# A gated linear-attention stage on one core: inner states kept by strips of two heads, one copy of the inner gate, variance as two float32r products

## The reference

```
xn = layernorm(x)
# gated linear attention, 16 heads, key size 16, value size 32
y  = rmsnorm(xn) ; q = y@Wq ; k = y@Wk * 32**-0.5 ; v = y@Wv ; g = y@Wg + bg
gk = logsigmoid(y@Wkg1@Wkg2 + bkg2) / 16          # Wkg1 is 512x16: the inner gate
S_t = S_{t-1} * exp(gk_t) + k_t v_t ;  o_t = q_t S_t     # per head, over the tokens
o  = (o - mean(o)) * rsqrt(var(o) + 1e-5)          # per head, over its 32 values
xm = xn + (silu(g) * o) @ Wo
s  = xm + (silu(rmsnorm(xm)@W1) * (rmsnorm(xm)@W3)) @ W2     # hidden size 1408
# a second branch from xn: softmax-weighted low-rank experts, then silu -> gate
out = x + s * gate
```

## Time and profile before

| | |
|---|---|
| median of 3 runs | 1599.29 us (1598.97 to 1599.48) |
| the profiled execution | 1597.72 us |
| its span, first to last instruction | 1596.0 us, granted TensorE clock 0.999 |
| PE busy | 1576.8 us (99%) |
| DVE busy | 847.4 us (53%), in stage A over 80% |
| ACT busy | 567.2 us (36%) |
| PE waits for another engine inside stage A | 0.4 us and 0.2 us |
| PE's wait for DVE's first inner gate, at the end of stage F | 0.19 us |
| from the ms subtraction (L1040) to the o0 addition (L1080), DVE, seven rows | 31.9 to 32.2 us |

### The profile page before, as it was taken

One profiled execution on the slowest core, in us unless ns is written; L12 is line 12 of the kernel. 1 busy time (PEld: TensorE's weight loads), 2 busy tenths in 40 slices (PEclk: granted clock), 3 DMA queues, 4 the chain that ended last, 5 costly groups with the idle time before them and its releaser, 6 DMA issues.

```text
span 1596.0 us, 30636 instructions
## 1 busy us (share of the span) xinstructions
PE 1576.8 (99%) x12274; PEld 1275.5 (80%) x12274; DVE 847.4 (53%) x1320; ACT 567.2 (36%) x988; POOL 162.5 (10%) x190
## 2 busy tenths in 40 slices
PE   7999999999999999999999999999999999999998
PEld 5888787787777777777777888888888888888887
DVE  5554555467797887978887451331415132241513
ACT  4333344276564655736555411111111111111111
POOL 1222331100221102201020100000000000000000
PEclk9999999999999999999999999999999999999999
DMA  7443442101020211202123423030300203030110
GB/s 160 142 101 92 119 112 73 60 28 42 22 87 3 87 43 47 87 3 87 61 82 123 142 96 136 0 138 0 138 0 30 108 0 138 0 138 0 63 44 27
DMA packets 50757, 114.08 MB, mean 71 GB/s; under 512 B 13322, under 2 KB 24666, under 8 KB 42467
## 3 DMA queue, kind: packets, MB, share of 16 engines
q1 hardware_dynamic: 47906, 99.95, 19.3%
q10 hardware_dynamic: 1152, 8.39, 1.3%
q0 software_dynamic: 1600, 4.25, 1.3%
HBM read 78.98 MB, written 33.59 MB: 71 GB/s over the span
## 4 chain that ended last, share of the span: by engine, by line
PE 90%; DVE 6%; ACT 1%; issue 1%; DMA 1%; SPq 1%; DVEq 0%; PEld 0%; ACTq 0%; PEldq 0%
PE m_ps L1569 9%; PE m_ps L1568 9%; PE m_ps L1567 9%; PE a_ps L161 7%; PE a_ps L163 7%; PE a_ps L162 7%; PE f_ps L161 6%; PE f_ps L163 5%; PE f_ps L162 5%; PE m_ps L1589 4%; PE m_ps L1590 4%; PE m_ps L1588 4%; PE a_att L1312 3%; PE a_ps L1431 2%; PE a_ps L1333 2%; DVE row L1843 1%
## 5 line engine op out<-in xcount | busy, mean ns | idle before, releaser
L1817 DVE TENSOR_TENSOR m_h<-m_ps,m_silu 128x512 f32<-128x512 f32 x85 | 58.7, 690 | 392.9 <-PE m_ps L1569 392.9
L1567 PE MATMUL m_ps<-m_xshi,m_w 128*128 128x512 f32 x680 | 266.2, 392 | 0.0
L1569 PE MATMUL m_ps<-m_xshi,m_w 128*128 128x512 f32 x680 | 264.7, 389 | 0.0
L1568 PE MATMUL m_ps<-m_xslo,m_w 128*128 128x512 f32 x680 | 264.6, 389 | 0.0
L1883 ACT ACTIVATE m_silu<-m_ps 128x512 f32<-128x512 f32 x85 | 50.7, 597 | 325.8 <-PE m_ps L1569 325.8
L1569 PEld LDWEIGHTS m_ps<-m_xshi,m_w 128*128 128x128 f32 x680 | 127.6, 188 | 26.6
L1567 PEld LDWEIGHTS m_ps<-m_xshi,m_w 128*128 128x128 f32 x680 | 127.7, 188 | 26.4 <-issue 0.2
L1568 PEld LDWEIGHTS m_ps<-m_xslo,m_w 128*128 128x128 f32 x680 | 127.7, 188 | 26.3 <-issue 0.2
L1045 DVE TENSOR_TENSOR a_a<-a_att,causal 128x1024 f32<-128x1024 f32 x64 | 75.2, 1216 | 11.8 <-PE a_att L1312 11.8
L1893 ACT ACTIVATE m_h0hi<-m_h 128x512 fp32r<-128x512 f32 x45 | 28.5, 633 | 132.0 <-DVE m_h L1817 132.0
L1588 PE MATMUL m_ps<-m_h0hi,m_w 128*128 128x512 f32 x188 | 73.1, 389 | 0.0
(11 more groups left out here) (318 smaller groups left out, 3484.5 us busy)
## 6 DMA issues: line engine op xcount, KB each, us to landing
row<-scratch_xn SPq DMA_DIRECT2D x16, 1024.0 KB, 4.8
row<-scratch_xmid SPq DMA_DIRECT2D x16, 1024.0 KB, 7.3
m_xt<-in_L_attn_W SPq DMA_DIRECT2D x33, 256.0 KB, 3.0
f_xt<-in_L_attn_x SPq DMA_DIRECT2D x32, 256.0 KB, 7.8
scratch_xn<-row SPq DMA_DIRECT2D x8, 1024.0 KB, 8.6
scratch_gate<-row ACTq DMA_DIRECT2D x8, 1024.0 KB, 3.9
scratch_xmid<-row SPq DMA_DIRECT2D x8, 1024.0 KB, 4.9
row<-scratch_gate SPq DMA_DIRECT2D x8, 1024.0 KB, 10.4
```

The costliest lines, as they stand in the source:

```text
L1567: pe.matmul(ps, wh, xh, start=k == 0, stop=False)
L1568: pe.matmul(ps, wh, xl, start=False, stop=False)
L1569: ins = pe.matmul(ps, wl, xh, start=False, stop=k == LAST)
L1817: dve.tensor_tensor(h[n], dense.region(f"b{j}"), silu[n], ALU.mult).then_inc(dense.taken_sem(f"b{j}"), 1)
```

## The change

- **States by strips.** `state` is 128 x 2 x 64 instead of 128 x 2 x 256: a strip of 32 partitions holds the two heads of that strip. State times query becomes eight products of 32 rows x 64 columns at tile positions (32*strip, 64*(strip % 2)), strips 0 and 1 into one bank, 2 and 3 into another. The mix has two banks (`a_mix`), in half of each. DVE's update is one masked copy of 128x128 and two steps of 128x64.
- **Transposed keys** go to the unused half of a mix bank (`turned`). For c = 1 and 2 they are made behind the projection instead of ahead of it, and the state products must wait until ACT has copied them.
- **Inner gate.** The weights hold three copies of the high part, so that four row blocks of u arise at once. ACT makes one copy (64x512), DVE one subtraction; before, DVE made three copies and the subtraction (16x512 each). The preparation of these weights on POOL changes with it.
- **Variance.** ACT squares into `sq`, ACT copies the high part into `og_hl[0]`, DVE subtracts for the low part (`squares_lo`), and TensorE adds two float32r products.
- **Gating.** `gated` is split: `weigh_out(c)` multiplies the silu gate with `oc`, and `gated` has three operations and runs two chunks on. ACT does `deviation` ahead of `inverse_deviation` in chunk 3.
- **Banks.** `dense` has two banks and, through a table `places`, the four attention banks for z, v1, v2, g0, g1, g2. The memsets of the attention banks (`clear_weights`) go. The loop's `head_slot` for TensorE goes.

```diff
-        psum = [... for b in range(4)]
+        psum = [... for b in range(2)]
+        ps_mix = ctx.enter_context(nc.psum_tensor("a_mix", [P, 2, 512], F32))[:]
+        places = {result: n for n, results in enumerate((
+            ["k0", "ds0", "var0", "q0", "ds2", "var2", "var3", "v3", "o0", "o2"],
+            ["k1", "u", "ds1", "var1", "q1", "ms", "v0", "g3", "o1", "o3"],
+            ["z0", "g0"], ["z1", "g1"], ["v1", "g2"], ["v2"])) for result in results}
+        turned = Regions(count, "kt", [ps_mix[:, ODD, GR * P:]], list(range(NC - 1)))
...
# DVE, inner gate
-                dve.tensor_copy(u[0:RANK], ps).then_inc(count.sem("uhi"), 1)
-                dve.tensor_copy(u[64:64 + RANK], ps).then_inc(count.sem("uhi"), 1)
-                dve.tensor_copy(u[96:96 + RANK], at.region("u")[32:32 + RANK]).then_inc(count.sem("uhi"), 1)
                 dve.wait_ge(*count.at("uhi", i))
-                dve.tensor_tensor(u[32:32 + RANK], ps, u[0:RANK].bitcast(F32), ALU.subtract)...
+                dve.tensor_tensor(u[low], at.region("u")[low], u[low].bitcast(F32), ALU.subtract)...
# ACT, inner gate
+                act.activation(u[0:4 * RANK], at.region("u")[0:4 * RANK], ACT.Copy).then_inc(count.sem("uhi"), 1)
# DVE, body
             for c in range(NC):
                 if c > 0:
-                    dve.wait_ge(*mix.ready(c - 1, i))
+                    squares_lo(i, c - 1)
                 ...                                   # ms low part (c = 3), masks, ahead
+                if c > 1:
+                    gated(i, c - 2)
                 ...                                   # state update
                 if c > 0:
-                    gated(i, c - 1)
+                    weigh_out(i, c - 1)
+            gated(i, NC - 2)
+            squares_lo(i, NC - 1)
+            weigh_out(i, NC - 1)
             ahead("gates")
             gated(i, NC - 1)
+        def weigh_out(i, c):
+            part = gsilu[:, :, tokens(c)]
+            dve.wait_ge(*dense.taken(f"g{LAST}", i))
+            dve.wait_ge(*mix.taken(c, i))
+            dve.tensor_tensor(part, part, oc, ALU.mult).then_inc(count.sem("og"), 1)
# ACT, body
+                if c == 1:
+                    squares(i, (2,))
                 for part in (("k0", "k1"), ("u",), ("q0",), ("q1",))[c]:
                     ahead(part)
+                if 0 < c < NC - 1:
+                    keys(i, c)
...
+                if c == NC - 1:
+                    deviation(i)
                 if c > 0:
                     inverse_deviation(i, c - 1)
-                if c == NC - 1:
-                    deviation(i)
                 act.wait_ge(*mix.ready(c, i))
-                act.activation(flat(sq), ps, ACT.Square).then_inc(count.sem("sq"), 1)
+                act.activation(by_quads(sq), ps, ACT.Square).then_inc(count.sem("squares"), 1)
+                act.wait_ge(*count.at("squares", i, 3 * c + 1))
+                act.activation(og_hl[0][:, :, tokens(c)], sq, ACT.Copy).then_inc(count.sem("squares"), 1)
# PE
-                pe.matmul(ps, avg32, flat(sq), start=True, stop=True)...
+                pe.matmul(ps, avg32.bitcast(F32R), og_hl[0][:, :, tokens(c)], start=True, stop=False)
+                pe.matmul(ps, avg32.bitcast(F32R), og_hl[1][:, :, tokens(c)], start=False, stop=True)...
...
+                    if 0 < c < NC - 1:
+                        pe.wait_ge(*mix.taken(c - 1, i))
+                        turned_keys(i, c)
                     if c > 0:
                         variance(i, c - 1)
...
+                    if 0 < c < NC - 1:
+                        pe.wait_ge(*turned.taken(c, i))
-                        for quad in range(QD):
-                            pe.matmul(ps[:, quad, :], state[c % 2][:, g, first_head * VH:...], qhat[:, gcs[g], :], ...)
+                        for g in range(GR):
+                            for strip in range(4):
+                                rows, at = slice(H32 * strip, H32 * (strip + 1)), H64 * (strip % 2)
+                                pe.matmul(ps[2 * g + strip // 2][at:at + H64], state[c % 2][rows, g, :],
+                                          qhat[rows, gcs[g], :], ..., tile_position=(H32 * strip, at))
```

More of the change, by code:

```diff
@@ L58, with __init__ @@
 class Regions:
-    def __init__(self, counts, name, regions, order, early=()):
+    def __init__(self, counts, name, regions, order, early=(), places=None):
         self.counts, self.name, self.regions = counts, name, regions
@@ L169, in loop, with loop_parts @@
     loop_parts(eng, n, {None: first}, lambda i, ahead: body(i, lambda: ahead(None)), peel)
-def loop_parts(eng, n, parts, body, peel=False, before=None, skip=None, first=True, slot=None):
+def loop_parts(eng, n, parts, body, peel=False, before=None, skip=None, first=True):
     for part, work in parts.items() if first else ():
@@ L182, in loop_parts @@
         body(0, lambda part: parts[part](1))
-    with eng.bass.Fori(1 if peel else 0, n - 1, engines=bass.OrderedEngineSet([eng.engine]), hint_back_edge=True,
-                       head_slot=None if slot is None else {eng.engine: slot}) as i:
+    with eng.bass.Fori(1 if peel else 0, n - 1, engines=bass.OrderedEngineSet([eng.engine]), hint_back_edge=True) as i:
         body(i, lambda part: parts[part](i + 1))
@@ L272, in prepare_attention_weights @@
     step(pool.memset(w["wkg2"].bitcast(F32), 0.0))
-    step(pool.memset(w["wkg1"].bitcast(F32), 0.0))
     RANK, KD = Wkg2.shape
-    small = w["stage"][0:RANK, 1, 0:KD]
+    small = w["stage"][0:4 * RANK, 1, 0:KD]
     sources = {"wkg1": Wkg1, "wk": Wk, "wq": Wq, "wv": Wv, "wg": Wg, "wo": Wo}
@@ L827, in phase_a @@
         kt_sb = flat(w["fold"]).rearrange("p (g t) -> p g t", g=GR)
-        state = [sb(f"state{n}", [P, GR, HG * VH]) for n in range(2)]
+        state = [sb(f"state{n}", [P, GR, 2 * VH]) for n in range(2)]
         sq, oc, rn = sb("sq", [P, QD, P]), sb("oc", [P, QD, P]), sb("rn", [P, QD, P])
@@ L845, in phase_a @@
                           ("decay", 1), ("m64", 3), ("m32", 3), ("mdk", 1), ("mdq", 2), ("mkh", 1), ("mqh", 1),
-                          ("state", GR * (NC - 2)), ("first", NC - 1), ("weighing", NC),
-                          ("sq", NC), ("rn", NC), ("og", 2 * NC), ("oghi", NC), ("oglo", NC)):
+                          ("state", GR * (NC - 2)), ("weighing", NC),
+                          ("squares", 3 * NC), ("rn", NC), ("og", 2 * NC), ("oghi", NC), ("oglo", NC)):
             count.add(name, per)
@@ L1218, in deviation, with keys, by_quads @@
                 act.activation(added[0:1], added[0:1], ACT.Exp, scale=-0.5).then_inc(count.sem("r2"), 1)
+            def keys(i, c):
+                act.wait_ge(*turned.ready(c, i))
+                act.activation(flat(kt_sb), turned.region(c), ACT.Copy).then_inc(turned.taken_sem(c), 1)
+            def by_quads(ap):
+                return ap.rearrange("p (g b) t -> p g b t", b=2)
             def body(i, ahead):
@@ L1230, in body @@
-                    for part in (("k0", "k1"), ("c1",), ("q0",), ("q1",))[c]:
+                        act.activation(og_hl[0][:, :, tokens(c)], square, ACT.Copy).then_inc(count.sem("x2parts"), 1)
+                    if c == 1:
+                        squares(i, (2,))
+                    for part in (("k0", "k1"), ("u",), ("q0",), ("q1",))[c]:
                         ahead(part)
+                    if 0 < c < NC - 1:
+                        keys(i, c)
                     if c == 0:
                         act.wait_ge(*dense.taken_before(f"o{LAST}", i))
-                    squares(i, ((0, 1), (2,), (3,), ())[c])
+                        squares(i, (0, 1))
@@ L1275, in first_row @@
                 elif part == "lent":
-                    for name in ("k0", "k1"):
+                    for name in ("u", "k0", "k1"):
                         parts[name](0, first)
@@ L1419, in body @@
                     if c > 0:
-                        for quad in range(QD):
-                            g, first_head = quad * HQ // HG, quad * HQ % HG
-                            pe.matmul(ps[:, quad, :], state[c % 2][:, g, first_head * VH:(first_head + HQ) * VH],
-                                      qhat[:, gcs[g], :], start=quad == 0, stop=True, skip_group_check=True)
+                        for g in range(GR):
+                            for strip in range(4):
+                                rows, at = slice(H32 * strip, H32 * (strip + 1)), H64 * (strip % 2)
+                                pe.matmul(ps[2 * g + strip // 2][at:at + H64], state[c % 2][rows, g, :],
+                                          qhat[rows, gcs[g], :], start=g == 0, stop=True, skip_group_check=True,
+                                          tile_position=(H32 * strip, at))
                     if c + 1 < NC:
@@ L1465, in tensor @@
             f.tensor(pe, first_row)
-            pe.wait_ge(s_mean8, 1)
-            for part in ("v0", "v1", "g"):
+            pe.wait_ge(s_parity, 4)
+            parts["v0"](0)
+            for m in range(KT):
```

(8 more changed lines are left out.)

161 lines of the change are left out of this document (76 added, 85 removed).

## The result

The changed kernel takes **1613.44 us** (1612.49 to 1613.70, 4 runs), the kernel before 1599.24 us (4 runs) beside it: ratio 1.0088, 95% interval 1.0075 to 1.0100. It is slower by 14 us. The forecast was 1601.3 and its range ended at 1608, so the time lies 5.4 us above the range.

What follows compares the result with a forecast made beforehand. The prediction took TensorE to bound the kernel. Its terms, -0.3 (stage start), -0.6 (first row), 6 x 0.13 (middle rows) and +2.1 (last row), sum to +2.0 us on 1599.29: 1601.3 us, range 1591 to 1608.

Steps and rivals of the forecast that it cites:

- The waits for the key copy: Chunks 1 and 2: state times query waits until ACT has copied the transposed keys, 0.4 us named in each chunk.
- at ms: Chunk 3: the mean-square product waits for ACT to empty the bank of q1, 0.5 us a row.
- at the fourth variance: Chunk 3: TensorE waits for DVE's low part of the squares, `squares_lo(3)`, 0.56 us a row.
- at o2: Output products: o2 takes o0's bank and waits for DVE's addition of o0, 1.03 us a row.
- The strips' query: State times query as eight strip products: 0.52 us with the change of shape, saving 0.47 three times a row.
- The two float32r products: Variance: two float32r products take 0.46 us instead of 0.85 for one float32 product, 0.39 saved four times a row.
- savings go into waits of DVE's string: Each row: about 2.6 us saved on TensorE goes into waits, those at variance 3 and o2 for DVE's operations.
- the two terms of the sum for row 0 and the last row: Edges of stage A: 0.6 us gained in the first row, 2.1 us lost in the last.
- the wait for `squares_lo(3)`: Last row, chunk 3: TensorE waits 3 us for DVE's low part of the squares before the fourth variance.
- The rival that came true: More small waits than named, or a cost of the loop's start without slot: +2 to +5 us, 1603.5 to 1606.5; chance 0.26.
- The eight products running two at a time: State times query: strips run two at a time and take 0.99 us as before; +9.5 in sum, 1608.8; chance 0.10.
- DVE's string shorter by a microsecond: End of a row: o2 does not wait, seven rows gain 1.03 us each; 1594.1, down to some 1587; chance 0.26.

Runs made afterwards that it cites:

- e9: The changed kernel with neither the strips (state times query on the full array again) nor the float32r variance (one float32 product): 1603.82 us, ratio 1.0032.
- e7: The changed kernel with the variance as one float32 product, without ACT's copy of the squares and DVE's `squares_lo`; strips kept: 1603.43 us, ratio 1.0022.
- e15: The changed kernel with the variance as one float32 product, but ACT's copy of the squares and `squares_lo` left in as unused work: 1611.37 us, ratio 1.0077.
- e2: The kernel before without the slot of TensorE's loop start, nothing else: 1600.60 us, ratio 1.0009.
- e13: The kernel before with TensorE's loop start in slot 224 instead of 163, nothing else: 1614.91 us, ratio 1.0100.
- e16: The changed kernel with strips, the variance as one float32 product and TensorE's loop start in slot 24: 1601.24 us, ratio 1.0020.

## Why the prediction was wrong

**The middle rows: right, nearly to the tenth.** The waits for the key copy, for ds1, at ms, at the fourth variance and at o2 are all there. The gates start at 533.06, less 4.67 is 528.39 (forecast 528.31); DVE adds o0 at 552.94 (forecast 553.08, before 552.63). Only the wait at o2 is 0.44 instead of 1.03, since TensorE comes 0.34 us later than forecast (553.24 for 552.90) and goes on 0.25 earlier. The body was forecast at 65.83 and is 65.72.

**Two sizes in it were off.** The strips' query takes 0.60, not 0.52, against 0.98 for the four full products of the kernel before, so the gain is 0.38 and not 0.47 a chunk. By e9 and e7 a row gains 1.03 and not 1.4 us. The two float32r products were to save 0.39 us each time, with 0.46 for the two. They take more, 0.71 in chunk 1 (510.68 to the end at 511.39) for 0.95 of the plain product in e7 (574.25 to 575.20). By the busy time of the middle rows (63.88 after, 64.71 in e7) about 0.2 is saved each time. In chunks 1 and 2 not even that counts: from the key transposes to state times query it is 1.17 and 1.18 us in e7, with the plain product, and 1.11 to 1.17 after.

**What the forecast had as its mechanism held, and what it left undrawn was the point.** I had written that savings go into waits of DVE's string. That is shown by e15 and e7. I had not asked what the same forecast says of the kernel without the r-variance: 2.4 us less DVE work a row, and no wait left. In e7 the gates come 0.9 us earlier and the middle rows have no wait. This part of the change was taken as a saving of 1.6 us a row, and it costs 0.9.

**The edges: the step that failed.** The step is the two terms of the sum for row 0 and the last row, in which waits for instructions stood at nothing. Forecast were -0.3 and -0.6 us at the start of the stage and in row 0, and +2.1 in the last row; measured -0.6, +5.3 and +11.1 (the last with stage M). The terms I had named were there: the wait for `squares_lo(3)` was 3.0 as forecast, o0 starts 13.79 us after variance 2 (forecast 12.45; the 1.3 us between them fit the stretch of lower clock behind the wait), o2 waits 1.1. Missing were the issue waits, 2.3 and 4.9 us, and what the timelines show behind them: DVE's string pushed under POOL's scaling in row 0 with 1.9 us of wait for ACT, and the three stretches of lower clock, up to 5.1 us. By e7, 4.9 of the 11.1 us go with the r-variance; 6.2 stay, with issue waits of 5.0 us and no stretch of lower clock. The first number holds only roughly, since the slots alone move this part between 778.3 and 782.5.

**The rival that came true was priced too low.** "The loop's start without its slot costs something, which the trace of before can't price" stood in a case of +2 to +5 us with a chance of 0.26. The size was too small. The kernel before shows that the slot itself was worth 1.4 us (e2). But the same code moved by other edits is another matter: the trace of before could have told that 84 packets came in nine a row, that 256 instructions of block products run in 1.62 us, and so that any edit that shifts the code of this engine can cost a microsecond or two in each chunk. e13, the old kernel with one number changed, is 16 us slower. The range should have reached further up for that.

**The other rivals.** The eight products running two at a time did not happen (0.60 us). That rival had named a rule of the Trainium skill, PSUM — Partial Sum Buffer, section on bank collisions, that different row tiles are not able to access one bank at the same time. The strips of different rows and columns in one bank ran in 0.60, not 0.99, so that rule did not slow them here. DVE's string shorter by a microsecond did not happen in the changed kernel, and did in e7.

**What stays open.** The last row with stage M keeps 4.4 to 8.7 us at every slot tried, while the old order has 0.4 to 2.0 there. The time is idle time of TensorE: in e16 TensorE is busy for 766.2 of 779.7 us, in the kernel before for 766.9 of 773.8. In e16's last row it waits 4.6 us for instructions at block products, 0.4 us under the same name at state times query, and 2.0 us for DVE's masked weights and ACT's squares, with the granted clock at 1.00; the kernel before has 0.3 us of waits for another engine there. Why the new order has more issue waits at the edges than the old one, and whether the waits for DVE and ACT follow on them, is open: no run had the new order without issue waits.

## What to carry to other kernels

When an engine runs a dense stretch of small instructions, its instruction fetch is a resource like a DMA queue: look at the instruction queue's packets and at waits named issue before an edit, and try the loop start at several places after it, for a comparison of two versions at one place each can be off by 1%. The name issue alone is no proof: look for the packet 2 to 3 us ahead. A saving on the engine that bounds is worth nothing if it is paid with work on the engine that is next: take each part out alone, and take the dead work out too. First and last passes have waits and code of their own; they held all of the added time here, while the middle rows only gained nothing.

## What the hardware showed that I had not expected

A loop of TensorE whose instructions lie in eight blocks of 256 was not fetched again: no packet of the instruction queue between 430 and 800 us after, nine a row before. The Trainium skill, Runtime: NRT & Kernel Launch, section Instruction fetch mechanics, gives TensorE 2048 instructions in blocks of 256, and our counts agree with that; it also says that the fetch is hidden behind the pace of issue, and there the runs decide otherwise, with 40 waits of 0.8 to 2.0 us.

To run from such a loop into the code behind it isn't free: in the changed kernel the first fetch since row 0 starts 0.9 us ahead of the last row's first product, and TensorE waits 1.08 us for it until 828.44.

Four scans of DVE that take 1.37 us together took 4.54 us with POOL at work beside them.
